# Attention steps that carry the rest of the batch: next q and k, output projection, similarities and expert work between them, and expert numbers summed by TensorE

## The reference

```python
q, k, v = heads(x @ w_qkv.T)
q, k = rope(rms_norm(q) * q_norm_w, rms_norm(k) * k_norm_w)
attn = softmax(where(causal, -inf, q @ k.T * scale))
x = layernorm(x + (attn @ v) @ w_proj.T)
xn = rms_norm(x) * norm_w
q2 = xn @ w_q.T                            # 8 heads, two halves of 128
s1, i1 = top_k(sim1, 8); s2, i2 = top_k(sim2, 8)     # over 32 keys each
fs, pk = top_k(s1[..., :, None] + s2[..., None, :], 8)
fi = (i1 * 32 + i2)[pk]                    # expert numbers, 0 to 1023
hidden = gelu(xn . expert_down[fi]) * relu(fs)
x = layernorm(x + sum(hidden * expert_up[fi]))
```

## Time and profile before

| | us |
|---|---|
| median of 3 runs | 1782.3 (1781.9 to 1787.96) |
| profiled execution, its own time | 1787.43 |
| span of the profiled execution | 1785.5 |
| busy: PE, DVE, ACT, POOL | 1353.2, 1507.0, 938.5, 750.4 |
| mean granted clock of TensorE | 0.818 |

### The profile page before, as it was taken

How to read it: one execution, slowest core, us unless ns; L and a number is a source line. 1 busy time by engine, 2 the same in 40 slices (tenths; PEclk the granted TensorE clock), 3 DMA queues, 4 the chain that set the end, 5 groups by cost and what they waited for, 6 DMA issues and landing times. The chain is left out here.

```text
span 1785.5 us, 53337 instructions
## 1 busy us (share of the span) xinstructions
PE 1353.2 (76%) x19632; PEld 929.3 (52%) x19632; DVE 1507.0 (84%) x6821; ACT 938.5 (53%) x1646; POOL 750.4 (42%) x1088
## 2 busy tenths in 40 slices
PE   3557588787968778796877869697887869688556
PEld 2323265554646555464645646474655546465436
DVE  2136898989899898989989899998989998988994
ACT  0647463755556475564647465564737555563110
POOL 1216353444635353453525355463534446352320
PEclk7688879797888879788887969888796978878665
DMA  3000000000000000000000000000000000000000
GB/s 77 1 6 8 6 8 8 14 8 1 15 7 15 7 14 8 1 15 7 15 7 14 8 2 15 6 15 7 15 8 14 8 1 15 1 15 1 8 7 9
DMA packets 29976, 18.59 MB, mean 10 GB/s; under 512 B 1824, under 2 KB 29216, under 8 KB 29728
## 3 DMA queue, kind: packets, MB, share of 16 engines
q1 hardware_dynamic: 29728, 15.23, 3.0%
HBM read 11.04 MB, written 4.19 MB: 9 GB/s over the span
## 5 line engine op out<-in xcount | busy, mean ns | idle before, releaser
L585 ACT ACTIVATE prob<-S 128x512 f32<-128x512 f32 x640 | 367.0, 598 | 298.8 <-PE OV L790 160.4
L869 PE MATMUL G<-whot,onehot 128*128 128x16 bf16 x12288 | 378.4, 172 | 48.3 <-DVE hid L1266 27.6
L869 PEld LDWEIGHTS G<-whot,onehot 128*128 128x128 bf16 x12288 | 365.7, 100 | 81.5 <-issue 23.5
L1228 DVE TENSOR_TENSOR onehot<-lo_no,esel 128x1024 bf16<-128x1024 uint16 x512 | 373.9, 785 | 0.2 <-issue 0.2
L422 POOL TENSOR_TENSOR qk_a<-qk_n,cosw 128x256 f32<-128x256 f32 x64 | 59.4, 928 | 482.6 <-DVE qk_n L1047 446.6
L839 PE MATMUL F<-xn,downT 128*128 128x512 f32 x256 | 153.9, 758 | 96.1 <-ACT hid L530 96.1
L777 PE MATMUL S<-causal,ident_b 128*128 128x128 bf16 x1024 | 209.1, 236 | 2.3 <-issue 2.3
L468 POOL TENSOR_TENSOR gat<-gat,cande 128x1280 f16<-128x1280 f16 x64 | 151.4, 2366 | 110.4 <-DVE gat L1189 110.4
L775 PE MATMUL S<-qT,kT_even 128*128 128x512 bf16 (+3 forms) x512 | 154.1, 332 | 50.9 <-ACT prob L585 42.3
L727 PE MATMUL S<-ident_b,stack 128*128 128x128 bf16 x1024 | 94.6, 261 | 106.1 <-POOL stack L438 72.9
L1169 DVE FIND_INDEX8 topi<-topv,sims 128x8 uint16<-128x32 f32 x1024 | 166.2, 185 | 0.0
(11 more groups left out here) (136 smaller groups left out, 2608.6 us busy)
## 6 DMA issues: line engine op xcount, KB each, us to landing
xa<-in_L_attn_x SPq DMA_DIRECT2D x16, 256.0 KB, 2.8
xr<-in_L_attn_x SPq DMA_DIRECT2D x16, 256.0 KB, 2.9
out<-r SPq DMA_DIRECT2D x16, 256.0 KB, 2.9
onehot<-in_L_ffn_expert_down SPq DMA_DIRECT2D x1, 512.0 KB, 5.9
up<-in_L_ffn_expert_up SPq DMA_DIRECT2D x1, 512.0 KB, 7.0
onehot<-in_L_ffn_keys SPq DMA_DIRECT2D x1, 256.0 KB, 6.3
onehot<-in_L_attn_w_qkv SPq DMA_DIRECT2D x1, 192.0 KB, 4.7
onehot<-in_L_attn_w_proj SPq DMA_DIRECT2D x1, 64.0 KB, 4.6
```

The source lines that it names most:

```text
L585: act.activation(dst, src, ACT.Exp, scale=SCALE).then_inc(exp_done.sem, 1)
L869: last = nc.tensor.matmul(bank[:, 16 * i:16 * i + 16], onehot[:, pair, t, :], whot[:, t, w_part, :], start=(w_part == 0), stop=(w_part == 2))
L1228: dve.tensor_tensor(onehot[:, pair, t:t + 8, :].rearrange("p t (c i) -> p t c i", i=2), lo, e, ALU.is_equal)
```

## The change

TensorE's order becomes one list of 40 steps with everything else hung on a step. A pass now does, between the scores of `b`: at step 1 the last `attend` of `late` = b-1, v of `b` itself and xT of `nxt`; at steps 2 and 3 `expert_outputs` of `oldest` (now into G1, two tiles a time) and q, k of `nxt`; at 4 the output projection of `late` and all `hidden_products` of `older`; at 8 yi of `late`; at 9, 11, 17, 21 its similarities; from 5 to 38, all but 21 and 31, all 32 parts of weights of `older`; at 25, 29, 33 and 39 the q and k transposes by head group instead of by row tile. S0 and S1 are shared out by one order over all uses (`S_ORDER`). The pipeline is one stage deeper: the output projection and first norm of a batch, and everything after, come one pass later, so that there is one more short pass at the end.

The expert numbers: GpSimd only multiplies (the fold, L471, is gone), and `turn_numbers` on TensorE turns and sums the 20 candidates at once at steps 22, 27, 32 and 35, 20 products each. VectorE's `selected` is gone. Squares of both halves feed one inverse root per pass, shared with both norms (140 columns wide); GpSimd rotates q and k before they are scaled, and VectorE scales after it. `r2`, `o`, `oT` and `yi` no longer share storage; `onehot` has 6 chunks, of which two are used twice.

```diff
-        SIMS_UNIT = 4
-        SELECTION_STEP = 34
-        WEIGHT_STEPS = list(range(1, 9)) + list(range(13, 29))
+        QK_STEPS = [25, 29, 33, 39]
+        SIMS_STEPS = [9, 11, 17, 21]
+        NUMBER_STEPS = [22, 27, 32, 35]
+        SELECTION_STEP = 36
+        WEIGHT_STEPS = [n for n in range(5, 39) if n not in (21, 31)]
...
+            def turn_numbers(b, t):
+                rows = slice(t % 2 * 64, t % 2 * 64 + 64)
+                pe.wait_ge(gat_done.sem, gat_done.value(b, t + 1))
+                if t == 0:
+                    pe.wait_ge(sims_done.sem, sims_done.value(b, 3))
+                for c in range(NCAND):
+                    last = nc.tensor.matmul(F_SEL[rows, t // 2 * P:(t // 2 + 1) * P], gat[:, t % 2, c].rearrange("p h k -> p (h k)"),
+                                            ident_b[:, :], start=(c == 0), stop=(c == NCAND - 1),
...
@@ TensorE, iteration @@
                 for step in range(NG * UNITS):
                     g, u = step // UNITS, step % UNITS
                     if b is not None:
-                        scores(b, g, [u])
+                        scores(b, g, [u], nxt)
                         if u == 1 and g:
                             attend(b, g - 1)
+                    if step == 1:
+                        if late is not None:
+                            attend(late, NG - 1)
+                        if b is not None:
+                            project_v(b, nxt)
+                        if nxt is not None:
+                            transpose_x(nxt, b)
+                    if step == 2:
+                        if oldest is not None:
+                            expert_outputs(oldest, range(2))
+                        if late is not None:
+                            transpose_o(late, NG - 1)
+                    if step == 3:
+                        if nxt is not None:
+                            project_qk(nxt, 0, b)
+                            project_qk(nxt, 1, b)
+                        if oldest is not None:
+                            expert_outputs(oldest, range(2, NT))
+                        if late is not None:
+                            turn_outputs(late)
+                    if step == 4:
+                        if late is not None:
+                            project_out(late)
+                        if older is not None:
+                            hidden_products(older)
                     if older is not None and step in WEIGHT_STEPS:
-                        weights(older, 8 + WEIGHT_STEPS.index(step))
+                        weights(older, WEIGHT_STEPS.index(step))
+                    if step == 8 and late is not None:
+                        transpose_yi(late)
+                    if b is not None and u == 3 and g:
                         transpose_o(b, g - 1)
...
@@ ScalarE, iteration: one exponential per n, and @@
+                    if n == 10:
+                        if late is not None:
+                            similarities(late, 0)
+                            norm1_rows(late)
+                        if oldest is not None:
+                            norm2_rows(oldest)
...
+                    if nxt is not None and n in (13, 14):
+                        first_parts(nxt, n - 13)
+                    if nxt is not None and n in (16, 17):
+                        second_parts(nxt, n - 16)
...
@@ GpSimd, iteration @@
+                if older is not None:
+                    keep_rows(older)
+                if nxt is not None:
+                    rotate(nxt, 0)
+                    rotate(nxt, 1)
+                    rests(nxt, 0)
+                    rests(nxt, 1)
                 if late is not None:
                     candidates(late, 0)
+                if nxt is not None:
+                    third_parts(nxt, 0)
+                    third_parts(nxt, 1)
...
```

More of the change, by code:

```diff
@@ L268, in attention_then_peer_layer @@
         A_USES += [("oTn", [(oTn_done, 1)]), ("proj", [(ln1, 1)])]
[L270 to L278, removed]
+        S_ORDER = [("scores", n) for n in range(NG * UNITS)]
+        QK_STEPS = [25, 29, 33, 39]
+        for g in reversed(range(NG)):
+            at = S_ORDER.index(("scores", QK_STEPS[g])) + 1
+            S_ORDER[at:at] = [("Q", g), ("K", g)]
+        for step, two in ((3, [("qk", 0), ("qk", 1)]), (1, [("v", 0), ("xT", 0)])):
+            at = S_ORDER.index(("scores", step)) + 1
+            S_ORDER[at:at] = two
+        S_READ = {"scores": exp_done, "v": v_done, "xT": xT_done, "qk": sq_done, "Q": qT_done, "K": kT_done}
         def pass_wait(eng):
@@ L651, in iteration @@
[L651 to L667 removed]
+                        exps(b, n // UNITS, [n % UNITS])
@@ new lines, in iteration @@
+                    if n == 4 and older is not None:
+                        for c in range(NHI):
+                            hidden(older, c)
+                    if n == 9 and late is not None:
+                        normed(late)
+                    if n == 10:
[4 more added lines that the diff above has]
+                            norm2_rows(oldest)
@@ L669, in _ @@
+                    if n == 22 and b is not None:
+                        attended(b, 1)
+                    if n == 23 and late is not None:
+                        similarities(late, 3)
+                    if n == 32 and b is not None:
+                        attended(b, 2)
+                    if nxt is not None and n in QK_STEPS:
+                        transposed(nxt, QK_STEPS.index(n))
             iteration(None, None, None, None, 0)
@@ new lines, in project_qk @@
+            def project_qk(b, half, last):
+                if half == 0:
+                    pe.wait_ge(xT_done.sem, xT_done.value(b, 1))
+                wait_s_empty(pe, last, b, "qk", half)
+                for i in range(2):
+                    t = 2 * half + i
+                    done = nc.tensor.matmul(bank_s("qk", half)[:, 2 * i * D:2 * (i + 1) * D], xT[:, t * P:(t + 1) * P],
+                                            wqkvT[:, 0:2 * D], start=True, stop=True)
+                done.then_inc(qk_ready.sem, 1)
@@ L931, in iteration @@
-                if nxt is not None:
-                    transpose_stack(nxt, 2)
-                if late is not None:
-                    for part in range(0, 4):
-                        weights(late, part)
-                if nxt is not None:
-                    transpose_stack(nxt, 3)
-                if late is not None:
-                    for part in range(4, 8):
-                        weights(late, part)
+                    if nxt is not None and step in QK_STEPS:
+                        transpose_stack(nxt, QK_STEPS.index(step), b)
@@ L1281, in iteration @@
                 if late is not None:
-                    top_pairs(late, 1)
-                    selected(late, 0)
                     top_keys(late, 3)
-                if b is not None:
-                    normalise_o(b, 0)
+                    top_pairs(late, 2)
                 if older is not None:
@@ L1346, in iteration @@
[L1346 to L1357 removed]
+                    one_hots(range(8))
```

699 lines of the change are left out of this document (326 added, 373 removed).

## The result

The changed kernel takes 1939.0 us (1938.5 to 1939.7, four runs) against 1783.1 us (1781.9 to 1788.0): a ratio of 1.087, interval 1.085 to 1.089. The profiled execution has a span of 1936.6 us. The forecast was 1806 us, the range 1694 to 1880: slower as forecast, but 133 us more than forecast, and outside the range.

A forecast was written before the change was run, and what follows sets the result against it. VectorE was taken to set the period: 89.1 us of work plus waits 1.9, 3.0, 1.1 and 10.9 give 106.0 against 101.9. Span 325 + 14 T is 1809, median 1806 us; range for 8 in 10, 1694 to 1880.

The forecast's parts named there:

- the ends: Filling and emptying around the steady loop: first decode at 187 us (bounds 175 and 200), 69 from batch 15's decode to the end.
- VectorE's work: VectorE's pass without waiting for anybody: 89.1 us, down from a period of 101.9; busy time near 86 a pass.
- Start: Start of VectorE's pass, where TensorE's expert products, q and k hold it up: waits of 1.9 us (bounds 0 and 4).
- candidates: VectorE waiting for GpSimd's `candidates(late, 0)`, queued behind both `rests`: 1.1 us (bounds 0 and 4).
- Similarities: VectorE's wait between yi and the copies of similarities, chunk 1 included: 3.0 us (bounds 1 and 6).
- The tail: Chain from `apply_weights` 4 through weights, `attend(b, 2)` and number products to the selection: VectorE waits 10.9 us (bounds 8.5 and 16).
- forecast's own sign: VectorE waits some 10 us a pass for the selection at `decode`'s first instruction; if absent, the tail term and forecast failed.
- point 4: The tail term of the walk through VectorE's waits: 10.9 us, from `apply_weights` 4 to the selection.
- 325 + 14 T: Span from filling, passes and end, T being the steady period; with T = 106.0 it gives 1809 us.
- VectorE hardly held up: Rival: start, similarities and candidates waits vanish (6.0 us) and two microseconds of collisions go; T = 98, median 1694; chance 0.32.
- the clock falling in the tail: Rival: the tail's whole chain at 1.2 GHz; T = 111, median 1876 us; chance 0.20.
- TensorE's dense order: Rival: TensorE bounds the pass at about 92 us, with all waits on S0 and S1 covered; chance 1 in 20.

The follow-up runs named there:

- Experiment 1: Changed kernel with ScalarE's first copy of similarities put ahead of exponential 10, nothing else moved; 1934.3 us, ratio to the kernel before 1.083.
- Experiment 5: Changed kernel with a spare tile for each group's first exponential, so exponentials 10, 20 and 30 don't wait for the attention just ahead; 1888.4 us, ratio 1.058.
- experiment 8: Changed kernel with VectorE work a pass altered behind the last one-hot writes: -1.2, +1.2, +2.4, +3.6 us; 1938.9, 1976.6, 1990.3, 1992.4 us.
- experiment 7: Scores of some units computed several times to keep TensorE busy: two versions on the changed kernel, 1939.4 and 1944.4 us, one with every wait moved, 1882.6.
- Experiment 4: Changed kernel with one number product per tile instead of 20, sums over candidates left out; 1925.1 us, ratio to the kernel before 1.078.
- +1.2 us of experiment 8: Changed kernel with one more VectorE reduction a pass behind the last one-hot writes; 1976.6 us, period 116.0 in eight passes, 114.1 to 114.8 in four.
- the last of experiment 7: Version with norm rows, similarities, candidates, spare tile and `apply_weights` 4 moved, scores of units 8 and 22 computed fifteen and eight times; 1882.6 us.
- second version of experiment 6: Changed kernel with norm rows, similarities' copy and candidates moved ahead, and `apply_weights` 4 ahead of `top_pairs` 2; 1883.1 us, period 109.1.
- experiments 1, 2, 7 and 8: The second of these: changed kernel with similarities' copy ahead of exponential 10 and GpSimd's candidates 0 and 1 moved ahead; 1933.9 us, period 112.65.

## Why the prediction was right or wrong

**Where the 133 us are.** The time is 1939.0 for 1806. The period's 6.6 us over 14 passes are 93 of them, the ends 35, and the step from the span to the median 5.6: 3.2 us were taken off, and the median lies 2.4 above the profiled span.

**VectorE's work: right.** Busy time is 85.1 us a pass where about 86 was forecast; 112.6 less the waits leaves 88, where 89.1 stood. Of the four one-hot writes inside the root three took 1.2 us and one 0.68, near the dear end of what was weighed.

**Start, candidates: right in size.** 2.3 for 1.9 and 0.3 for 1.1, within their bounds.

**Similarities: the step that failed.** "Because ScalarE's order has exponential 10 in front, 0.6": I priced the exponential and not what it waits for. It waits for `attend(b, 0)`, which TensorE does at step 11, behind a step with similarities and a step with scores and weights. 9.5 us for 3.0, beyond the bound of 6. Experiment 1 moved the copy ahead of it and the wait fell to 4.1, so 5.4 of the 6.5 too much are this wait. The other 1.1 is the size of what the clock cost on the way: the walk priced the similarity product at full clock, 0.97 us, and it took 2.04 at half. The forecast looked for a falling clock in the tail only, but the longest stretch at half clock, 13.6 us, lies around yi. Experiment 5 took the wait away from the first exponential of every group and the time fell by 51 us. The period was missed by 6.6 us (112.6 for 106.0); this term is 6.5 more than forecast, and the others nearly cancel: tail 1.7 and start 0.4 more, candidates 0.8 and VectorE's work 1.1 less.

**But a wait's length was not its price.** Experiment 1 removed 5.4 us of it and got 4.7 us in 1939. Three other waits grew by 5.2, one of them because an attention that had run at full clock ran at half. The steps of experiment 8 are of the same sort, and no sum of waits can see them. So the walk's term names the place truly, and a sum of such terms doesn't give the period here.

**The tail: right in kind, 12.6 for 10.9.** VectorE waits for o and the selection, TensorE for `hid` ahead of chunk 6; moving one `apply_weights` gave 41 us. By the forecast's own sign, some 10 us of wait at `decode`, point 4 would have failed: that wait is 3.7. The chain is the one that was priced, but VectorE meets it first at the division of o, 6.8, and at chunk 6, 2.1; the sign named the wrong instruction. The excess is `attend(b, 2)` at half clock: 2.0 us more, of which I had taken 1. The 20 number products take 1.30 us, 0.065 each, as taken from the transposes (0.066); the next product starts 1.24 us after the first of them, 0.062 each. By the 55.6 ns of the Trainium skill (TensorE: Matmul & The Clock Gate, section Wait — 56ns, not 53.3ns?) they would be 1.1 us, an estimate; the row, at full clock, decides for the dearer.

**Ends.** With the measured period the formula 325 + 14 T gives 1902; the span is 1936.6. The 35 us between, term by term: the first decode at 205.8 and not 187 (18.8 more); batch 1 at 110.7 and not T - 4 = 108.6 (2.1); batch 14 at 103.7 and not T - 13 = 99.6 (4.1); batch 15 at 93.7 and not 86 (7.7); the end at 71.0 and not 69 (2.0). The first attention pass took 58 us (56 forecast), but then 7 us pass before batch 1's first exponential, and the second pass has its decode at 74 us and not 66, by waits of the same sort as in the steady loop (9.3 us for the similarities).

**The rivals.** The first, VectorE hardly held up, is refuted: its three short waits are 12 us together. The second, the clock falling in the tail, is partly there (the first 5.4 of the tail's 17.4 us are at half clock), but keeping the clock up there gave nothing (experiment 7). The third, TensorE's dense order as the bound with the waits covered, is refuted by the busy times: TensorE idles for 25.6 of 112.6 us. Experiment 4 adds little, as its clock fell too.

**What is shown and what isn't.** Shown: the mean period of most versions of the changed kernel is one of four values 3.4 us apart (105.8, 109.2, 112.6, 116.0). Two are not: +1.2 us of experiment 8, and the last of experiment 7 with 108.8. Single passes need not be at the mean: the second version of experiment 6 repeats 108.5, 108.9 and 110.3. Shown too: two gains that are each a step give one step together; and in experiments 1, 2, 7 and 8 a gain elsewhere came with `attend(late, 3)` at half clock, 1.2 to 1.7 us longer. Not shown: why the falls settle so that the period is kept. So the cause of the term that was mis-sized is shown, and what sets the period in the end stays open. It is a reading, not a result, that this is so because fp32 attention products stand in the chain in four places of a pass, 2.3 us at full clock and up to 4.4 at half, and TensorE is idle ahead of several of them. The kernel before is nearest to VectorE's bound, and its time rises with VectorE's work instead. Whether full double buffering of `prob` would lift the changed kernel further was not tried. No version beats the kernel before; the best that computes all is at 1883 us, and it would need about two more steps.

## What to carry to other kernels

When a copy is priced behind another instruction in an engine's queue, price what that instruction waits for, above all the release of a buffer with one copy: here that was 7.15 us, where the instruction itself was 0.6. When the sum of busy times is well under the period on every engine and the clock changes within a pass, test the period's slope before trusting any sum: add and remove a microsecond on one engine. Where it goes in steps, a small gain can show nothing alone, and two can show no more than one: try them together before you drop either.

## What the runs showed of the hardware

Less work for TensorE came with a lower granted clock in experiment 4: without 76 products a pass it was 0.803 over the run against 0.838, and 0.79 and 0.78 against 0.86 in the two passes shown, where busy time stayed at 86 to 89 us. More work raised it, from 0.838 to 0.883 over the whole run with three stretches filled, and the time did not fall. In the changed kernel's steady loop the clock's falls come at the same places of both passes looked at (915.5 and 1028.1, 973.5 and 1086.2), within 0.2 us; 1.2 us less work for VectorE moved time not at all, 1.2 us more cost 38 us, and 3.6 us more cost 53.
